# A fused patch-embedding, attention and expert layer: set-up reordered, a dense copy of the image tile for the embedding's weight loads, and a new stage order

## The reference

```python
patches = patchify(x)                                   # (64, 121, 676)
emb = einsum('bnf,df->bnd', patches, W) + b + pos_emb   # (64, 121, 192)
h = fq_act(layernorm(tokens) @ fq_weight(w_qkv).T + b_qkv, s_a1)
attn = log_int_softmax(fq_act(einsum('bhnd,bhmd->bhnm', q, k) * Dh**-0.5, s_attn), s_attn)
o = fq_act(fq_act(einsum('bhnm,bhmd->bhnd', attn, v), s_a2) @ fq_weight(w_proj).T + b_proj, s_a3)
scores = softmax(xt @ gate_w + gate_b)                  # groups of two, 4 groups, then 4 experts
y = sum_e weight_e * (silu(xt @ Wg_e + bg_e) * (xt @ Wu_e + bu_e)) @ Wd_e + shared + residual
```

## Time and profile before

| what | value |
|---|---|
| median of 3 runs | 3578.61 us |
| lowest and highest | 3577.92 and 3579.04 us |
| profiled execution, its own time | 3582.08 us |
| its span (first to last instruction) | 3580.2 us |
| TensorE busy | 3401.8 us (95%) |
| VectorE busy | 3420.2 us (96%) |
| ScalarE busy | 3164.2 us (88%) |
| GpSimd busy | 873.5 us (24%) |
| mean granted TensorE clock | 0.990 |

### The profile page before, as it was taken

How to read it: one execution, slowest core, us unless ns; L and a number is a source line. 1 busy time by engine, 2 the same in 40 slices (tenths; PEclk the granted TensorE clock), 3 DMA queues, 4 the chain that set the end, 5 groups by cost and what they waited for, 6 DMA issues and landing times. The chain is left out here.

```text
span 3580.2 us, 98075 instructions
## 1 busy us (share of the span) xinstructions
PE 3401.8 (95%) x30764; PEld 2894.2 (81%) x30764; DVE 3420.2 (96%) x10281; ACT 3164.2 (88%) x6226; POOL 873.5 (24%) x1646
## 2 busy tenths in 40 slices
PE   0589999999999999999999999999999999999999
PEld 0368888888888888888888888888888888888888
DVE  5589999999999999999999999999999999999995
ACT  1689999999999999999999999999999999999992
POOL 3122222222222222222222222222222221222220
PEclk9889999999999999999999999999999999999999
DMA  5000000000100100010000010011000000001000
GB/s 122 20 14 23 25 19 22 25 22 19 26 25 16 26 25 16 25 25 18 22 25 21 20 25 24 17 26 25 16 25 25 17 24 25 20 21 25 22 13 8
DMA packets 157124, 85.77 MB, mean 24 GB/s; under 512 B 51452, under 2 KB 154371, under 8 KB 156611
## 3 DMA queue, kind: packets, MB, share of 16 engines
q1 hardware_dynamic: 153692, 78.82, 8.9%
q10 hardware_dynamic: 2918, 0.67, 0.1%
HBM read 54.89 MB, written 12.24 MB: 19 GB/s over the span
## 5 line engine op out<-in xcount | busy, mean ns | idle before, releaser
L1165 PE MATMUL pU<-x2T,UG 128*128 128x250 f16 x8704 | 1226.9, 270 | 0.1
L1165 PEld LDWEIGHTS pU<-x2T,UG 128*128 128x128 f16 x8704 | 818.3, 97 | 118.5 <-DVE work L1006 0.8
L1191 PE MATMUL pY<-WD,work 128*128 128x192 f32 (+1 forms) x4352 | 812.1, 329 | 0.1
L1191 PEld LDWEIGHTS pY<-WD,work 128*128 128x128 f32 (+1 forms) x4352 | 690.8, 187 | 8.5 <-DVE work L1011 0.5
L945 DVE SCALAR_TENSOR_TENSOR work<-work,cst 128x249 f32<-128x249 f32 (+1 forms) x1536 | 669.7, 491 | 11.6 <-issue 7.0
L607 ACT ACTIVATE work<-work,alpha 128x249 f32<-128x249 f32 (+1 forms) x1536 | 646.1, 502 | 1.3 <-DVE alpha L957 0.9
L591 ACT ACTIVATE work<-a,room 128x249 bf16<-128x249 int8 (+1 forms) x1536 | 644.2, 502 | 0.2 <-POOL room L505 0.2
L1165 PE MATMUL pU<-x2T,UGB 67*128 67x250 f16 x2176 | 592.4, 272 | 0.0
L616 ACT ACTIVATE passing<-pX,cst 128x512 int16<-128x512 int16 (+3 forms) x768 | 477.4, 681 | 4.7 <-PE pX L1117 4.7
L925 DVE TENSOR_REDUCE rmax<-a 128x4 f32<-128x996 int8 (+1 forms) x384 | 451.9, 1177 | 25.0 <-ACT a L582 24.7
L966 DVE SCALAR_TENSOR_TENSOR work<-work 128x996 bf16<-128x996 bf16 (+1 forms) x384 | 453.6, 1181 | 0.0
(11 more groups left out here) (209 smaller groups left out, 5356.8 us busy)
## 6 DMA issues: line engine op xcount, KB each, us to landing
img<-in_x_dram SPq DMA_DIRECT2D x896, 23.5 KB
img<-in_x_dram SPq DMA_DIRECT2D x768, 21.4 KB
qz<-qb SPq DMA_DIRECT2D x768, 15.6 KB, 1.8
h<-in_txt_dram SPq DMA_DIRECT2D x64, 96.0 KB, 1.9
out_dram<-yout SPq DMA_DIRECT2D x64, 96.0 KB
out_dram<-yout SPq DMA_DIRECT2D x64, 90.8 KB
WD<-in_L_ffn_Wd_dram SPq DMA_DIRECT2D x1, 1536.0 KB, 7.9
work<-in_L_ffn_Wu_dram SPq DMA_DIRECT2D x2, 512.0 KB, 7.5
```

What stands on the lines that cost most here:

```text
L1165: a = mm(pU[:, s, q * EVEN:(q + 1) * EVEN], weights, x2T[i % 2][0:w, m, 0:EVEN], start=m == 0, stop=m == BLOCKS - 1)
L1191: a = mm(pY[0:n, t * 256:t * 256 + D], (act_[k % 2] if k else up[0])[:, c:c + n], WD[:, e, :], start=k == 0 and t == 0, stop=e == E - 1, s ...
```

## The change

It has four parts.

1. **Image tile.** A new ScalarE stage `flat` copies the used columns of `img` (847 values on 116 partitions, read with a step of 13) into `imgc`, laid out as seven dense blocks of 121. `embed` takes its stationary operand from `imgc` and waits for `flat`; the next image's load waits for `flat` and no more for `embed`.
2. **Order.** `ORDER` has the same 254 stages and `flat`, in another order with other shifts: `project`, `prq`, `residual`, `stats2`, `mean2` stand near the table's end with shift -2 where they stood at its start with -3, most of the first experts' steps have moved into shift -4, and three of six units' `expo` were in shift -1 where now two are.
3. **Start on SP.** The first image and text are loaded ahead of the 51 `UGB` rows; the wait for those rows has moved from TensorE's start to its first expert matmul.
4. **Set-up.** GpSimd clears `tokW_cols` first and `img`, `h`, `UGB` later; VectorE takes the qkv weights last; ScalarE scales all four expert tiles (two of them VectorE's before), ahead of the qkv transposes.

The diff, without the table:

```diff
+        imgc = cut(CPAIRS * PATCHES).rearrange("p (m t) -> p m t", m=CPAIRS)
...
+        by_offset = img[0:CROW + CK].rearrange("p a b -> p (a b)").rearrange("p (t k) -> p k t", k=K)[:, 0:K:2, :]
...
         ORDER = [
-            ("vq", -2, -1), ("outq", -3, 2), ("outcast", -3, 2), ("grow", -2, 0), ("quant", -2, 4),
+            ("below", -2, 2), ("quant", -2, 4), ("quot", -2, 2), ("embed", -1, -1), ("sum", -2, 0),
...
+            sp.wait_ge(s_gsetup, 4)
+            load_image(0)
+            load_text(0)
             sp.wait_ge(s_bparts, 1)
             for s in range(SPLIT):
                 for e in range(E1):
                     load(ld_late, UGB[REST + s:REST + s + 1, e, :, :], b_parts[e:e + 1, s, :, :])
-            sp.wait_ge(s_gsetup, 1)
...
-                    if stage == "imgload":
-                        hold(emb, i)
+                    if stage == "imgload" and i:
+                        hold(flat_done, i)
+                        load_image(i)
...
-            for a in (qk_bias, w_rows, p_rows, bd_rows, img, h[0], h[1]):
+            for a in (qk_bias, w_rows, p_rows, bd_rows):
...
-            for a in (identf, ident, ident16, tokW_cols, p_int, v_add, p_add, GW, UGB):
+            for a in (tokW_cols, identf, ident, ident16, p_int, v_add, p_add, GW):
...
+            for a in (img, h[0], h[1], UGB):
+                nc_.memset(a[:], 0.0)
...
+            for n in range(TOK_JOBS):
+                move(n)
+            for b, (signal, n) in enumerate(((ld_f0, 5), (ld_f1, 10), (ld_f2, 5))):
+                act.wait_ge(signal, 16 * n)
+                sc_.activation(UG[:, b], ug_rows[b][:], ACT.Copy, scale=LIFT).then_inc(s_ug, 1)
...
+                    if stage == "flat":
+                        act.wait_ge(img_in, 16 * 2 * K * (i + 1))
+                        after(act, emb, i)
+                        sc_.activation(imgc[0:CROW + CK], by_offset, ACT.Copy).then_inc(flat_done, 1)
...
-                link(ts(UG[:, b], ug_rows[b][:], LIFT, None, ALU.mult))
+                dve.wait_ge(s_ug, 1 + b)
...
-            pe.wait_ge(s_asetup, PSETUP + 2)
-            pe.wait_ge(s_vsetup, VSETUP)
-            pe.wait_ge(s_gsetup, 7)
-            pe.wait_ge(ld_late, 16 * E1 * SPLIT)
+            pe.wait_ge(s_asetup, PSETUP)
+            pe.wait_ge(s_gsetup, 8)
...
-                        pe.wait_ge(img_in, 16 * 2 * K * (i + 1))
+                        pe.wait_ge(flat_done, i + 1)
...
-                            a = mm(pX[0:PATCHES, 0:D], img[0:n, :, 2 * c:2 * c + (PG - 1) * K + 1:K],
+                            a = mm(pX[0:PATCHES, 0:D], imgc[0:n, c, :],
...
+                        if k == 0 and i == 0:
+                            pe.wait_ge(ld_late, 16 * E1 * SPLIT)
+                            pe.wait_ge(s_ug, 4)
```

More of the change, by code:

```diff
@@ L330, in fused_layer @@
[L330 to L339, removed]
@@ new lines, in fused_layer @@
+            ("r_part0", -4, -1), ("alpha", -2, 0), ("mmG", -4, 0), ("gate", -4, 0), ("r_rest", -4, -1),
+            ("embed_h", -1, -1), ("power", -2, 2), ("spread2", -3, -1), ("silu", -4, 1), ("u", -2, 2),
+            ("mmU", -4, 2), ("below", -2, 3), ("norm2", -3, -1), ("quot", -2, 3), ("r_part1", -4, -1),
+            ("square", -2, 2), ("stats", -1, -1), ("mmG", -4, 1), ("score", -2, 5), ("r_part2", -4, -1),
+            ("sum", -2, 1), ("chosen", -4, -1), ("mean", -1, -1), ("down", -4, 0), ("gate", -4, 1),
@@ new lines, in fused_layer @@
+            ("qkq", -1, 1), ("power", -2, 3), ("grow", -2, 1), ("act", -4, 2), ("below", -2, 5),
+            ("weigh", -2, 1), ("qk", -1, 2), ("expo", -2, 3), ("low", -2, 2), ("below_max", -3, -1),
+            ("sum", -2, 3), ("pick", -4, 3), ("qkq", -1, 2), ("mmU", -4, 5), ("power", -2, 4),
+            ("store", -5, -1), ("alpha", -2, 3), ("qk", -1, 3), ("down", -4, 2), ("square", -2, 4),
+            ("qkq", -1, 3), ("qk", -1, 4), ("quot", -2, 5), ("imgload", 0, -1), ("silu", -4, 5), ("act", -4, 3),
@@ new lines, in fused_layer @@
+            ("alpha", -2, 4), ("sum", -2, 5), ("score", -1, 0), ("turnp", -2, 1), ("quant", -1, 0),
+            ("copyp", -2, 1), ("mmG", -4, 6), ("act", -4, 4), ("share", -2, 4), ("down", -4, 3),
+            ("silu", -4, 7), ("score", -1, 1), ("qk", -1, 5), ("down", -4, 4), ("qkq", -1, 5), ("pick", -4, 5),
+            ("grow", -2, 3), ("weigh", -2, 2), ("top", -1, 0), ("peak", -1, 0), ("alpha", -2, 5),
+            ("r_sum", -3, -1), ("value", -2, 0), ("weigh", -2, 3), ("v", -1, -1), ("mmU", -4, 8),
@@ new lines, in fused_layer @@
+            ("outcast", -2, 0), ("top", -1, 2), ("peak", -1, 1), ("below", -1, 1), ("outq", -2, 1),
+            ("down", -4, 7), ("r_penalty", -3, -1), ("score", -1, 3), ("peak", -1, 2), ("quot", -1, 1),
+            ("copyp", -2, 5), ("value", -2, 4), ("qzload", -1, 2), ("outcast", -2, 1), ("r_masked", -3, -1),
+            ("act", -4, 8), ("r_top", -3, -1), ("power", -1, 1), ("value", -2, 5), ("silu", -3, 0),
+            ("expo", -1, 0), ("quant", -1, 3), ("down", -4, 8), ("outq", -2, 2), ("outcast", -2, 2),
@@ L355, in fused_layer @@
+            ("u", -1, 1), ("vconv", -1, -1), ("top", -1, 3), ("result", -4, -1), ("project", -2, -1),
+            ("prq", -2, -1), ("flat", 0, -1), ("residual", -2, -1), ("r_take", -3, -1), ("square", -1, 1),
+            ("stats2", -2, -1), ("txtload", 0, -1), ("mmU", -3, 1), ("score", -1, 4), ("expo", -1, 1),
+            ("mean2", -2, -1), ("peak", -1, 3), ("r_weight", -3, -1),
         ]
```

122 lines of the change are left out of this document (66 added, 56 removed).

## The result

The changed kernel takes 3554.46 us (median of 4 runs, 3552.79 to 3556.15), and beside it the kernel before 3578.82 us (4 runs, 3577.92 to 3582.03): ratio 0.993, 95% interval 0.9913 to 0.9948. It is faster by 24.4 us, where 66 were forecast. The sign and the range held, the size did not.

A forecast was written before the change was run, and what follows sets the result against it. VectorE was taken as the bound. 59 periods of 52.03 instead of 52.93 us gave -53, start -14, filling -7, emptying +8: -66, span 3514.2, median 3512.6 us; own range 3490 to 3535, wider range 3475 to 3556.

The forecast's parts named there:

- Order: VectorE's stage order: from six direct pairs to one, 0.55 us off each period, with nothing added to VectorE in the steps.
- (c): VectorE instructions stretched under GpSimd: three places, 0.6 us a period; a fifth, 0.12, counted as gained.
- direct pairs: VectorE stages waiting for the one directly ahead: 0.11 us lost each, six pairs, 0.66 us a period.
- the rule weighed in the prediction: Trainium skill: a semaphore between chained VectorE instructions costs nothing extra; the order would then save 0.25 a period, not 0.80.
- Embedding: TensorE's fourteen passes with dense weights: 3.42 to 2.29 us, 1.13 us a period gained; VectorE gains only 0.13.
- (b): VectorE's wait at `embed_h` for TensorE's embedding: 0.13 us a period, counted as gained.
- `flat`: ScalarE's strided copy: 1.0 us, bounds 0.98 and 1.66, hidden while the period is longer than ScalarE's 50.0 us.
- Rival B: Slower: `flat` delays ScalarE's last `square` and VectorE behind it; decides from 4.15 us; at 5.0 us, 3629 us; chance 0.07.
- Start and filling: Before image 4: first score at 98.7, 12.9 us gained; -14 us to `h` of image 1, then -7 to image 4.
- Emptying: After the last `h`: +8 us, bounds -3 and +14, from 14 for experts' pairs, less 5 and 1.
- A: Rival: the period barely changes, as the pairs' cost turns up elsewhere in waits between engines; 3559 us, chance 0.12.
- C: Rival: everything VectorE loses is won back, period 51.4, 3478 us; chance 0.11.

The follow-up runs named there:

- the dense run: The changed kernel with `flat` reading the first 847 values of each image row one after the other instead of every thirteenth: 3554.15 us, ratio 0.9928.

## Why the prediction was wrong in size

**What bounds the kernel** was right: VectorE, 299.25 of 300 us, and in the best runs over 299.4.

**Order** is the step that failed, in "Nothing was added to VectorE in the steps" and "Of (c) I take a fifth away ... by chance of where GpSimd's work falls". Neither holds. The direct pairs gave 0.09 to 0.13 each, and the new one, `prq` to `residual`, costs 0.12, which bears out the row and not the rule weighed in the prediction: here a stage that waits for the one directly ahead of it pays for that. Whether it is the semaphore or the dependence that costs isn't separated, and a stage with another one in between pays nothing, though it waits on a semaphore too. (c) gave more than my fifth: the `expo` rows over 0.5 us lay 0.46 us a period above 0.47 in all, now 0.25, and `r_pairs` gave another 0.17 that the sum didn't have. But the new table put a `sum` and a cast under GpSimd's split passes, +0.74 and +0.33 us a period, the same in every period. What I took for a stretching by chance is a wait that follows from form and place, and which stages stand around `split2` could be read in the two tables; that it was at work in the kernel before stood in the rows of `r_pairs`. Of the 0.66 us a period that the forecast of 52.03 was short, the moved `sum` brings back 0.53 (52.16). For the 0.13 left there are several takers: the wait for `project` (+0.13 on `result`), the cast (+0.33), and the 0.13 that the router's subtraction costs more since the `sum` is gone. Moving the cast brought 0.07. Which of them it is was not separated.

**Embedding**: 2.28 us (1535.23 to the next row at 1537.51), 2.29 forecast:

```profile
1535.23 2.44 PE L1082 MATMUL pX<-tokWT,work 116*121 116x192 f32 x14
1537.51 0.59 PE L1190 MATMUL pU<-x2T,UG 128*128 128x250 f16 x4
```

Its worth to VectorE, (b) 0.13, was the old table's. In the new one the copy is worth 62 us, as the run without it shows: (3449.98 - 278.79) / 59 = 53.75 a period against 52.69. The sum came out no worse for it, because the new table without the copy would have been slower by as much; table and copy aren't two terms that can be added.

**`flat`**: 1.68 us, not 1.0, and beyond my bound of 1.66. The 0.77 us of it that the dense run took away cost nothing, as forecast, but not for the reason given. It isn't ScalarE's total slack that hides it. With the copy at the end of the old table 1.7 us of ScalarE cost 1.0 us a period (53.96 against 52.93), while ScalarE was busy for 282.74 of 300 us. Rival B had the right kind of mechanism (a late ScalarE stage ahead of a chain), and my point of decision at 4.15 us was wrong: it depends on the place.

**Start and filling**: -23.5 us in all where -21 were forecast, and to the first score by the queue as forecast. It came at 97.81 (98.7 forecast), with the q copies as its releaser:

```profile
97.81 1.02 PE L1118 MATMUL pS<-kb,qz 128*128 128x249 bf16 x4 [15.26 <-DMA qz<-qb]
```

VectorE's set-up had ended at 61.30. From the first score to `h` of image 1 it took 22.35 us, where the prediction's 26.7 less 1.1 are 25.6; no run looked at why. **Emptying**: +8.1 for +8, with the residual of image 63 at 3479.03, 72 us ahead of the end. That it came out so close is luck: behind that residual TensorE is busy for 65.1 us in place of 56.1, +9.0 where the experts' pairs were put at +14, and its idle time there went from 7.2 to 6.9 where 5 us less were expected.

Of the rivals, A (3559 us) came nearest in time and was wrong in mechanism: VectorE stands idle for 0.75 of 300 us, less than the 1.56 of before; it is the instructions that are longer. That the range held is luck in this sense: the time lies 4.5 us from A's, and the range took in the better half of A, whose cause isn't the one found. C (51.4 a period) wasn't reached by any run: with `sum` and cast moved the period stays at 52.09.

## What to carry to other kernels

When an order changes, lay the two engines that share a port beside each other: list GpSimd's instructions, and look which casts, `tensor_scalar` and instructions with two SBUF inputs of VectorE fall under them. A four-value instruction cost 0.82 us there, busy shares don't show it, and one place in the table was worth 34 us. Price a copy on an engine with slack by who stands behind it at that place, and an engine's gain by every consumer behind it in the new order, not only by the direct one. After mending one such place, read the trace again: the neighbours move under the same instruction.

## What the runs showed of the hardware

- A VectorE `tensor_scalar` of 128x4 float32 took 0.58 us under GpSimd's two-input subtraction and 0.16 beside it; a `tensor_reduce` of the same values 0.12 under it. A `gate` that reads PSUM (0.67 us) and batch statistics were not held.
- A VectorE `tensor_tensor` with both inputs in SBUF took 0.44 us, not 0.17, under GpSimd's cast, in 58 of 58 periods; in the kernel before another took 0.36 in 57 of 57, and 0.16 in the changed kernel where no cast lay over it. Such rows end within 0.04 us of GpSimd's, and no idle time shows.
- A VectorE stage of 0.16 us cost 0.19 from start to start when the stage behind it needed its result, and 0.08 otherwise.
- ScalarE's copy of 847 float32 values on 116 partitions took 0.91 us dense and 1.68 us with a step of 52 bytes, 1.07 and 1.98 ns a value.
- Fourteen float32 passes of TensorE took 2.28 us with dense stationary operands and 3.42 with a step of 52 bytes.
